# One decoder layer on Trainium2: first B and C and the last expert weights by matmuls, constants on two queues, one DMA per expert pair, and new places for the steps

## What is computed

```python
x = layernorm(x + mamba(x))              # 256 channels, 16 states, conv of 4 taps
x = layernorm(x + retention(x, ctx))     # q, k turned by xpos tables; decay mask in place of softmax
x = layernorm(x + moe(x))                # 16 experts of width 64, top 2 by the router, and a shared one

# the core of mamba, for every token t of a sequence:
xc = silu(conv(x @ W_in_x)); proj = xc @ W_xproj          # proj = (delta_raw, B, C)
delta = softplus(delta_raw @ W_dt + b_dt)
h = exp(delta * A) * h + delta * xc * B                   # for each of 16 states
y = sum_over_states(h * C) + D * xc;  out = (y * silu(z)) @ W_out
```

## Time and profile before

| what | value |
|---|---|
| three runs | 1181.36, 1184.04, 1192.93 us (median 1184.04) |
| profiled execution | 1200.76 us, its span 1198.9 us |
| mean granted TensorE clock | 0.963 |
| busy | PE 89%, DVE 89%, ACT 83%, POOL 81%; PEld 62% |
| DMA | 194.50 MB, 84112 packets, mean 162 GB/s |
| bc_all loads | 128 of 1024 KB, median 5.2 us from issue to landing |
| comb_all loads | 240 of 128 KB, median 3.2 us, and 32 of 64 KB |
| q_pair swaps | 30 of 128 KB, median 5.1 us; k_pair swaps 2.0 us |

### The profile page before, as it was taken

How to read it: one execution, slowest core, us unless ns; L and a number is a source line. 1 busy time by engine, 2 the same in 40 slices (tenths; PEclk the granted TensorE clock), 3 DMA queues, 4 the chain that set the end, 5 groups by cost and what they waited for, 6 DMA issues and landing times. The chain is left out here.

```text
span 1198.9 us, 18323 instructions
## 1 busy us (share of the span) xinstructions
PE 1065.9 (89%) x5831; PEld 742.7 (62%) x5831; DVE 1068.7 (89%) x1492; ACT 993.3 (83%) x2176; POOL 971.3 (81%) x590
## 2 busy tenths in 40 slices
PE   5667887989989898999989899998999999988897
PEld 2546565665756666665666657566666656666666
DVE  2999999898999999999998999999899999999622
ACT  6778797988879898888979889898988989797342
POOL 0677798887979898988988789798888979898754
PEclk8697989999999999999999999999999999999999
DMA  6444454445546454654645455464546546454322
GB/s 174 166 141 169 141 178 161 154 161 176 178 151 183 173 176 162 188 178 150 201 166 156 156 177 178 151 204 173 157 161 189 192 127 203 170 159 148 112 83 67
DMA packets 84112, 194.50 MB, mean 162 GB/s; under 512 B 17288, under 2 KB 47936, under 8 KB 67632
## 3 DMA queue, kind: packets, MB, share of 16 engines
q1 hardware_dynamic: 84016, 193.33, 48.7%
HBM read 179.14 MB, written 5.77 MB: 154 GB/s over the span
## 5 line engine op out<-in xcount | busy, mean ns | idle before, releaser
L936 POOL TENSOR_TENSOR read<-state,bc_all 128x1024 f32<-128x1024 f32 x256 | 603.3, 2362 | 74.6 <-DVE state L805 66.1
L805 DVE TENSOR_TENSOR_SCAN state<-decay,drive_bank 128x512 f32<-128x512 f32 (+1 forms) x464 | 597.2, 1316 | 17.7 <-POOL read L936 15.6
L755 ACT ACTIVATE decay<-delta,a_neg 128x252 f32<-128x252 f32 x1024 | 422.0, 494 | 0.9
L797 DVE TENSOR_TENSOR drive_bank<-dx_bank,bc_all 128x512 f32<-128x512 f32 (+1 forms) x496 | 329.0, 702 | 17.9 <-DMA bc_all<-bc_dram 17.7
L372 PE MATMUL y_bank<-ident,read 128*128 128x128 f32 x2048 | 283.0, 285 | 48.1 <-POOL read L936 47.2
L372 PEld LDWEIGHTS y_bank<-ident,read 128*128 128x128 f32 x2048 | 240.3, 146 | 127.4 <-POOL read L936 82.1
L977 POOL TENSOR_TENSOR hid<-gu,comb_all 128x512 f32<-128x512 f32 (+1 forms) x136 | 164.8, 1213 | 19.3 <-DVE gu L897 11.7
L363 PEld LDWEIGHTS down_bank<-down_w,hid 128*128 128x128 f32 x1024 | 131.7, 192 | 38.6 <-issue 34.7
L363 PE MATMUL down_bank<-down_w,hid 128*128 128x128 f32 x1024 | 136.5, 276 | 0.7 <-POOL hid L977 0.7
L363 PE MATMUL bank<-x2T,gate_w 128*128 128x512 f32 (+1 forms) x272 | 134.1, 585 | 0.8 <-DVE gu L897 0.2
L363 PE MATMUL bank<-x2T,up_w 128*128 128x512 f32 (+1 forms) x272 | 131.6, 577 | 1.6 <-DVE conv L765 1.3
(11 more groups left out here) (128 smaller groups left out, 1372.6 us busy)
## 6 DMA issues: line engine op xcount, KB each, us to landing
bc_all<-bc_dram SPq DMA_DIRECT2D x128, 1024.0 KB, 5.2
comb_all<-comb_dram SPq DMA_DIRECT2D x240, 128.0 KB, 3.2
x_in<-in_x_dram SPq DMA_DIRECT2D x15, 256.0 KB, 6.9
ctx_in<-in_ctx_dram SPq DMA_DIRECT2D x15, 256.0 KB, 3.3
k_pair<-k_pair SPq DMA_DIRECT2D x30, 128.0 KB, 2.0
q_pair<-q_pair SPq DMA_DIRECT2D x30, 128.0 KB, 5.1
out_dram<-y_out SPq DMA_DIRECT2D x15, 256.0 KB, 5.7
comb_all<-comb_dram SPq DMA_DIRECT2D x32, 64.0 KB, 2.6
```

What stands on the lines that cost most here:

```text
L755: done = e.activation(seqs(decay_t[j % DECAYS][:, i, h, :])[:, :, 1:T], seqs(delta[c % 2][:, h, sub * SUB:(sub + 1) * SUB])[:, :, 1:T], AC ...
L797: e.tensor_tensor(drive_bank[:, a:b, :, :], dx_bank[:, :, :].unsqueeze(1).to_broadcast(shape), bc_all[group % BC_BUFS][:, 0, PAIR * i + a: ...
L805: e.tensor_tensor_scan(states(state_t[j % STATE_BUFS], a, b), states(decay_t[j % DECAYS], a, b), states(drive_bank, a, b), 0.0, ALU.mult, ...
L936: e.tensor_tensor(read_t[j % READS][:, :, :, :], state_t[j % STATE_BUFS][:, :, :, :], bc_all[group % BC_BUFS][:, 1, PAIR * i:PAIR * (i + 1 ...
```

## The change

- Places: every group and every exp has its own place in five columns: the first chunk, the second, the middle ones, the last but one and the last. In the middle chunks a few groups move by some ticks; q_swap goes from 85 to 75, q_rot from 86 to 84, k_rot from 70 to 74, and xc0 and xc1 from -31 to -36 and -33, so that xc0 now stands ahead of dx_bank of the sub before.
- First B and C: the first group of B and C isn't loaded from DRAM. After dt_mm of the first chunk eight matmuls with a column of the identity spread rows of proj over the partitions (down_bank and y_bank), and four DVE instructions copy them to bc_all[0]. DVE also makes the first proj, and the first dx directly in dx_bank, which POOL and ACT did. The centring of w_out and down_w moves from tick -3 to 7.
- Constants: ident, a_log, conv_w and conv_b are issued by ACT's queue, all others stay on SP's, most of them later (ticks -15, -7 and 1), and there are more semaphores, so that an instruction waits only for its own constants. Three small activations load ACT's tables early.
- Last expert weights: for the last chunk eight matmuls with a selector take the weights from combT into the free banks of drive, dx and y. DVE makes hid there from gu and those banks; POOL's hid, the store and the loads of comb fall away for that chunk.
- One DMA per pair of experts, of both rows, where there were two.

```diff
+LAST = CHUNKS - 1
+COLUMN = [3, 4] + [0] * (CHUNKS - 4) + [2, 1]
...
-    "xT_mm": [(-45, -49)],
-    "q_copy": [(79, 68)],
-    "xc0": [(-31, -36)],
-    "xc1": [(-31, -23)],
-    "k_rot": [(70, 66)],
-    "q_rot": [(86, 79)],
-    "bc_store": [(-21, -29)],
-    "q_swap": [(85, 57)],
...
+    "xT_mm": [(-46, -46, -45, -64, -45)],
+    "q_copy": [(79, 71, 80, 45, 78)],
+    "xc0": [(-36, -32, -35, -37, -36)],
+    "xc1": [(-33, -26, -33, -18, -35)],
+    "k_rot": [(74, 65, 70, 32, 74)],
+    "q_rot": [(84, 68, 84, 62, 86)],
+    "bc_store": [(-31, -23, -27, -26, -33)],
+    "q_swap": [(75, 60, 75, 41, 75)],
...
+        def last_weight(pair):
+
+            if pair < PAIR * HALVES:
+                return drive_bank[:, pair // HALVES, pair % HALVES, :]
+            return dx_bank[:, pair % HALVES, :] if pair < PAIR * HALVES + 2 else y_bank[:, pair % HALVES, :]
+
...
+                place = SUB_TICKS * FIRST_SUB[c] + places[COLUMN[c]]
...
+                    w.wait_ge(S["tap_consts"], 16 * 2)
...
+                    if c == 0:
+                        for two in (0, 1):
+                            for pair in (0, 1):
+                                w.wait_ge(S["bc_copy"], 2 * two + pair - 1)
+                                for i in range(PAIR):
+                                    row = DT_RANK + GROUP * pair + PAIR * two + i
+                                    done = mm((down_bank, y_flat)[pair][:, i * SUB:(i + 1) * SUB],
+                                              ident[0:PROJ, row:row + 1].to_broadcast([PROJ, P]), proj[0:PROJ, 0:SUB])
+                                done.then_inc(S["bc_mm"], 1)
...
+                for c, pair in due(tick, "weight_mm"):
+                    if c < LAST:
+                        continue
+                    w.wait_ge(S["combT"], at(c))
+                    w.wait_ge(S["state"], PAIR * STEPS)
+                    w.wait_ge(S["y_gated"], ALL_SUBS)
+                    w.wait_ge(S["selector"], 1)
+                    mm(last_weight(pair), selector[0:EXPERTS, pair * P:(pair + 1) * P],
+                       combT[:, 0:SUB]).then_inc(S["weight_mm"], 1)
...
+            def warm(i, func):
+
+                e.activation(warmed[:, i:i + 1], eps_col[:, 0:1], func, scale=1.0)
+
+            e.dma_start(ident[:, :], io["c_ident"]).then_inc(S["ident"], 16)
+            e.dma_start(a_log[:, :, :], io["L0_attn_A_log"].rearrange("(h p) n -> p h n", p=P)).then_inc(S["a_log"], 16)
+            e.dma_start(conv_w[:, :, :], io["L0_attn_conv_w"].rearrange("(h p) k -> p h k", p=P)).then_inc(S["conv_consts"], 16)
+            per_channel(e, conv_b, io["L0_attn_conv_b"], S["conv_consts"])
+            w.wait_ge(S["zero"], DECAYS + 2)
+            warm(0, ACT.Exp)
+            w.wait_ge(S["a_log"], 16)
+            e.activation(a_exp[:, :, :], a_log[:, :, :], ACT.Exp, scale=1.0).then_inc(S["a_exp"], 1)
+            w.wait_ge(S["a_exp"], 1)
+            e.activation(a_neg[:, :, :], a_exp[:, :, :], ACT.Copy, scale=-1.0).then_inc(S["a_neg"], 1)
...
+            def bc_copy(two, pair):
+
+                w.wait_ge(S["bc_mm"], 2 * two + pair + 1)
+                e.tensor_scalar(bc_all[0][:, pair, PAIR * two:PAIR * (two + 1), :].rearrange("p n t -> p (n t)"),
+                                (down_bank[:, :], y_flat)[pair], 1.0, 1.0, ALU.mult, ALU.mult).then_inc(S["bc_copy"], 1)
...
+                for c in due(tick, "proj"):
+                    if c > 0:
+                        continue
+                    w.wait_ge(S["proj_mm"], 1)
+                    e.tensor_scalar(proj[:, 0:SUB], bank_of["proj", 0][0:PROJ, 0:SUB], 1.0, 1.0, ALU.mult, ALU.mult).then_inc(
+                        S["proj"], 1)
+                for c, sub in due(tick, "dx"):
+                    if c > 0:
+                        continue
+                    bc_copy(0, 0)
+                    w.wait_ge(S["delta"], 2)
+                    w.wait_ge(S["xc"], HALVES)
+                    e.tensor_tensor(dx_bank[:, :, :], xc[0][:, :, 0:SUB], delta[0][:, :, 0:SUB],
+                                    ALU.mult).then_inc(S["first_dx"], 1)
+                    bc_copy(0, 1)
+                    bc_copy(1, 0)
+                    bc_copy(1, 1)
+                    w.wait_ge(S["d_consts"], 16 * 2)
                     for h in range(HALVES):
+                        done = e.tensor_scalar(d_diag[:, h, :], ident[:, :], d_param[:, h:h + 1], 1.0, ALU.mult, ALU.mult)
+                    done.then_inc(S["d_diag"], 1)
...
-                        (0, -3, ((w_out[:, :, :], 0, HALVES), (down_w[:, :, :], HALVES, PAIRS))),
-                        (1, 5, ((w_qkv[:, 2:3, :], HALVES + PAIRS, 1), (shared_w[:, 2:3, :], HALVES + PAIRS + 1, 1)))):
+                        (0, 7, ((w_out[:, :, :], 0, HALVES), (down_w[:, :, :], HALVES, PAIRS))),
+                        (1, 15, ((w_qkv[:, 2:3, :], HALVES + PAIRS, 1), (shared_w[:, 2:3, :], HALVES + PAIRS + 1, 1)))):
...
+                for c, pair in due(tick, "hid"):
+                    if c < LAST:
+                        continue
+                    index = pair + 1
+                    w.wait_ge(S["gu"], at(c, index, TILES))
+                    w.wait_ge(S["weight_mm"], pair + 1)
+                    w.wait_ge(S["down_mm"], at(c, index - 3, TILES))
+                    e.tensor_tensor(hid[index % 3][:, 0:SUB], gu[index % 2][:, 0:SUB], last_weight(pair),
+                                    ALU.mult).then_inc(S["last_hid"], 1)
...
+                if tick == -15:
+                    for i, name in enumerate(("Wq", "Wk", "Wv")):
+                        e.dma_start(qkv_rows[:, i, :], io["L0_xattn_" + name]).then_inc(flips, 16)
+                    e.dma_start(router_rows[:, :], io["L0_ffn_router_w"]).then_inc(flips, 16)
+                    for i, name in enumerate(("sh_gate", "sh_up", "sh_down")):
+                        e.dma_start(shared_rows[:, i, :], io["L0_ffn_" + name]).then_inc(flips, 16)
+                    e.dma_start(w_out[:, :, :], io["L0_attn_W_out"].rearrange("(h p) n -> p h n", p=P)).then_inc(
+                        S["out_consts"], 16)
+                if tick == -7:
+                    e.dma_start(down_w[:, :, :], io["L0_ffn_down_proj"].rearrange("k e d -> (k e) d").rearrange(
+                        "(j p) d -> p j d", p=P)).then_inc(S["out_consts"], 16)
+                    e.dma_start(ctx_t[0][:, 0:blocks_of(0), :], rows_of(io["ctx_1024"], 0)).then_inc(S["ctx_load0"], 16)
+                    e.dma_start(xpos[:, :, :], io["c_xpos"]).then_inc(late, 16)
+                    e.dma_start(decay_mask[:, :], io["c_decay_mask"]).then_inc(late, 16)
+                    e.dma_start(router_bias[:, :], io["L0_ffn_router_bias"].rearrange("(a n) -> a n", a=1).partition_broadcast(
+                        P)).then_inc(late, 16)
+                    e.dma_start(expert_back[:, :], io["c_expert_back"]).then_inc(late, 16)
+                if tick == 1:
+                    e.dma_start(ctx_t[1][:, 0:blocks_of(1), :], rows_of(io["ctx_1024"], 1)).then_inc(S["ctx_load1"], 16)
+                    e.dma_start(gate_w[:, :, :], io["L0_ffn_gate_proj"].rearrange("k d e -> d k e")).then_inc(late, 16)
+                    e.dma_start(up_w[:, :, :], io["L0_ffn_up_proj"].rearrange("k d e -> d k e")).then_inc(late, 16)
...
-                    for i in range(2):
-                        row = comb_dram[c % 2][2 * index - 2 + i:2 * index - 1 + i, 0:width(c)]
-                        e.dma_start(comb_all[use % COMBS][i * EXPERT_DIM:(i + 1) * EXPERT_DIM, 0:width(c)],
-                                    row.to_broadcast([EXPERT_DIM, width(c)])).then_inc(COMB_LOAD[use % COMBS], 16)
+                    rows = comb_dram[c % 2][2 * pair:2 * pair + 2, 0:width(c)]
+                    e.dma_start(comb_all[use % COMBS][:, 0:width(c)],
+                                rows.unsqueeze(1).to_broadcast([2, EXPERT_DIM, width(c)])).then_inc(COMB_LOAD[use % COMBS], 16)
```

More of the change, by code:

```diff
@@ L100 @@
[L100 to L104, removed]
+    "xT_mm": [(-46, -46, -45, -64, -45)],
+    "tap_mm": [(-38, -37, -37, -50, -42)],
+    "xb_mm": [(-43, -42, -43, -56, -43)],
+    "proj_mm": [(-32, -23, -31, -26, -24)],
+    "dt_mm": [(-19, -19, -19, -12, -20)],
+    "ctxT_mm": [(62, 27, 61, 15, 57)],
+    "k_mm": [(69, 68, 69, 36, 69)],
+    "v_mm": [(68, 70, 68, 36, 62)],
@@ new lines @@
+    "out_mm": [(69, 69, 69, 42, 69)],
+    "q_mm": [(78, 71, 78, 43, 78)],
+    "r1_var_mm": [(86, 72, 83, 54, 86)],
+    "score_mm": [(94, 86, 96, 69, 94)],
+    "retout_mm": [(105, 91, 105, 74, 105)],
+    "x2T_mm": [(117, 97, 128, 92, 117)],
+    "router_mm": [(129, 102, 130, 96, 129)],
+    "combT_mm": [(136, 120, 136, 104, 136)],
+    "xT": [(-45, -45, -45, -52, -47)],
+    "conv_bias": [(-41, -41, -41, -47, -41)],
+    "proj": [(-24, -20, -27, -18, -32)],
+    "ctxT": [(59, 31, 59, 25, 58)],
@@ L288, in blocks_of, with loads @@
             return width(c) // P
+        def loads(buffer, groups):
```

(13 more changed lines are left out.)

254 lines of the change are left out of this document (136 added, 118 removed), and 5 rows, old and new, of the table EXP_AT.

## The result

The changed kernel takes 1477.12 us (median of 4 runs, 1474.52 to 1479.65) against 1188.49 us (1181.36 to 1194.15) of the kernel before beside it: ratio 1.243, 95% interval 1.235 to 1.252. It is 24% slower where I had forecast 1% faster.

The account below looks back on a forecast made before the run. It took a latency chain to bound the start, DVE the middle and PE the end. Gains of 2, 10 and 1 us, 13 in all, took 1184 us to 1171, with an 8-in-10 range of 1152 to 1192.

Parts of the forecast that it names:

- (b): Middle: one DMA per pair saves an issue, so DVE waits less for bc_all (17.7 us to near 12): 5 us won.
- the one on the single DMA: Middle: the merged load may land later than two halves, but three buffers give it the time of two hids.
- my rivals: Whole kernel: more won, 1153 us (chance 0.18); no change in the middle, 1181 (0.24); slower, 1196 (0.11).
- (a): Middle: earlier q_swap and q_rot, later k_rot remove most of DVE's 15.6 us wait for POOL's read: 15.6 - 2 us won.
- (c): Middle: xc0 with its table load ahead of dx_bank on ACT makes the drive wait: 8 us lost, between 0 and 14.
- rival "slower": Middle: xc0 waits for tap_mm on PE, so dx_bank is 2.4 us late in 14 chunks: 1196 us, chance 0.11.
- my own sign: Middle: prediction wrong if drive_bank's new wait for dx_bank exceeds 1 us in most chunks, or DVE's idle sum stays.
- The start: Up to the first drive: 23.7 us instead of 29.97, less 4.1 handed back for centring and a tap: 2 us won.
- The end: After the last scan: eight matmuls cost PE 3.7 us against credits of 1.4, 0.9 and 2.4: 1 us won.
- the credit of 4.7 us: End: PE's idle 1.4 us, 0.9 for comb load and hid, 2.4 for POOL's late read, set against the matmuls.
- The sum: Whole kernel: start 2, middle 10 and end 1 us, together 13 us won, giving 1171 us; chance 0.47.

Follow-up runs that it names:

- e3_wide: Changed kernel, one DMA per pair kept but its source's slowest dimension 64, not 2 (which weight meets which channel differs from the reference): 1167.42 us, ratio 0.978.
- e1_two: Changed kernel with the expert-weight load of a pair as two DMAs again, all else as changed: 1184.46 us, ratio 0.992 to the kernel before.
- e1b_two: Second run of e1_two's code (changed kernel, two DMAs per pair again): ratio 0.991 to the kernel before.
- e1c_two: Third run of e1_two's code (changed kernel, two DMAs per pair again): ratio 0.989 to the kernel before.
- e3b_wide: Second run of e3_wide's code (changed kernel, one spread DMA per pair), on one chip with e1c_two: ratio 0.982 to the kernel before.
- e5b_full: Second run of e5_full's code (whole layer, spread DMA, weights reordered), on another chip: ratio 0.981 to the kernel before.
- e5_full: Changed kernel with one spread DMA per pair and weights reordered by copies, so it computes the whole layer: ratio 0.991 to the kernel before.
- e12_best: As e5_full, but the last chunk's expert weights come by store and loads as before, not by matmuls: 1163.16 us, ratio 0.977 to the kernel before.

## Why the prediction was wrong

**The step that failed is (b)**, in the sentence "The bytes are the same and queue on the same engines", and with it the one on the single DMA that "has the time of two hids". The bytes are the same; the engines are 2, not 16. An estimate from rows shows how far this is from small: a middle chunk has eight pair loads at 5.2 us on those two engines, 42 us, and eight loads of 1 MB, of which each engine has 64 KB, at some 25 GB/s 2.6 us each, 21 us. That is 63 us in a chunk of 1095.4 / 16 = 68 us, near to DVE's own share. The chunk grew to 1336.0 / 16 = 84 us; that it grew beyond 68 because this work comes in bursts is argued, not measured. I looked at the cost of an issue (0.54 us) and never at what the issue sets going; none of my rivals had it, so the range did not reach it.

**(b)'s size, with the pattern right**: 5 us forecast, 9 to 11 measured by medians in two comparisons, 17 in one; DVE's wait for bc_all is 10.5 and 14.8 in the two runs of e3_wide where I wrote "near 12".

**(a)**: "with it most of the 15.6 us" was right of the wait and wrong of the time. By itself it won nothing, since y_bank and conv were late next; in the new order its absence costs over 50 us. I had asked only what DVE waits for, not what it would wait for then.

**(c)**: 8 us of cost forecast, 0 to 14. The changed kernel has 16.2, and xc0 at 579.33 also waited 0.33 us for PE, as in my rival "slower". All 11 waits are over 1 us, which by my own sign speaks against the prediction, as does DVE's idle time in the middle, which grew. In e1_two and e3_wide the wait is 0.7 and 1.2 us. There the new place used up slack and little else: in e3_wide dx_bank ends 0.4 us ahead of its drive in nine chunks, where the kernel before had 1.0 to 4.7 in the 13 middle ones. The chunk of the earlier trace rows was one of five with slack near 1.0, and I charged 14 chunks by it. Why ACT comes later in the changed kernel I did not test. A drain as on the Trainium skill's page ScalarE: Activation LUTs, section What ACT_TABLE_LOAD costs, would have made (c) dearer; the waits of the changed kernel fit the load of 1.28 us alone (577.72 to 579.00, and PE done for xc0 at 579.33).

**The start**: first drive forecast at 23.7, measured 22.7, in part by errors that cancel. The eight matmuls began at 13.88, not 15.1, and took 4.5 us (to 18.39), not 6; from their end to the drive it was 4.3 us, not 2.6, since DVE stood 1.74 us for ACT's conv, which I had left out. The centring fills DVE for 4.1 us from 30.16 on, and the tap at 25.00 takes 0.7 more, against 4.1 for both. Net 2.6 us won for 2.

**The end**: forecast 1 us won. In the nine kernels with matmuls and without the two-engine loads it took 73.2 to 76.4 us against 73.5: between nothing and 3 us lost. The price of the eight matmuls was right, 3.7 us both forecast and in e3_wide (1143.53 to 1147.24). What failed is the credit of 4.7 us against them: in the kernel before, PE is busy for 63.42 of the 64.6 us from 1125.4 to 1190, so after the last scans there was little idle time to win.

**The sum** without (b) would have been 8 us won; e1_two, e1b_two and e1c_two won 10 to 13; close, but in part by luck, since (a) was worth something else, (c) nothing there and the end a small loss. With the spread DMA the forecast 13 stands against 20 to 27 in three runs (e3_wide, e3b_wide, e5b_full) and 10 in e5_full.

## What to carry to other kernels

When a DMA's access pattern changes, read its slowest dimension before its bytes: merging two loads into one with a leading dimension of 2 turned 16 engines into 2, and everything that needs all 16 queued behind it. In a trace the sign is a flat DMA share near two sixteenths (0.13 at 51 GB/s from 1431 to 1434 us of the changed kernel) while a large load lands late. A wait that a profile puts down to "issue" may be one for an instruction that ended just before: look at what did. A wait removed from the pacing engine is worth its length only if nothing else is late next; one edit alone, in the old order and in the new, told more than the sum of waits.

## What was not expected of the hardware

In three of the thirteen profiles of the new order (e1c_two, e5_full, e12_best) TensorE ran at half pace from 11 to about 23 us while the granted clock stayed at 1.00 in the records. e1_two and e1c_two are the same code. In e1_two:

```profile
11.45 1.06 PE L399 MATMUL bank<-xc,w_xproj 128*40 128x256 f32 x4 [0.87 <-ACT xc L795]
```

and in e1c_two, with the window (columns as above):

```profile
11.23 1.93 PE L399 MATMUL bank<-xc,w_xproj 128*40 128x256 f32 x4 [0.87 <-ACT xc L795]
...
27.61 1.29 DVE L902 TENSOR_TENSOR drive_bank<-dx_bank,bc_all 128x512 f32<-128x512 f32 x2
```

```profile
13.00:19.00 6.00, 6.00 (x16) 4.18 (x16) 1.18 (x3) 3.21 (x6) 0.00 (x0) 1.00 0.39 104
```

The four matmuls take 1.93 us for 1.06, the first drive comes 5 us later, and the granted clock of the window says full speed (2.4 GHz). A start that is timed in one profile can be 5 us off by this alone. Whether it has a part in e5_full's 0.991 against e5b_full's 0.981 isn't shown: e12_best started as slowly in its profile and is at 0.977. What sets it off is open.

SP's issue of a DMA itself stretched to 5.88 us behind the two-engine loads, where 0.3 to 0.6 is usual.
